# One graph and mixture-of-experts kernel: sorted groups of 13 and 4 blocks in place of 12 and 5, with earlier fills, later first tiles, and sums issued between the last sends

## The reference

```python
x = x + relu(adj @ (item_feat @ W_item.T + b_item) + layernorm(x) @ W_user.T + b_user)   # adj is 10000 x 10000
z = layernorm(x)
probs = softmax(z @ gate_w + gate_b)             # 8 experts
cw = the two largest of probs, zero elsewhere
x = x + sum over e of cw[:, e] * (gelu(z @ W1[e] + b1[e]) @ W2[e] + b2[e])
```

## Time and profile before

| what | value |
|---|---|
| median of three runs | 1503.61 us |
| profiled execution, its own time | 1498.51 us |
| its span in the profile | 1496.7 us |
| PE busy | 1451.1 us (97%) |
| DVE busy | 1262.9 us (84%) |
| ACT busy | 1093.5 us (73%) |
| POOL busy | 712.5 us (48%) |
| moved by DMA | 489.21 MB, 327 GB/s on average |
| TensorE clock granted, mean | 0.998 |

### The profile page before, as it was taken

One profiled execution on the slowest core, in us unless ns is written; L12 is line 12 of the kernel. 1 busy time (PEld: TensorE's weight loads), 2 busy tenths in 40 slices (PEclk: granted clock), 3 DMA queues, 4 the chain that ended last, 5 costly groups with the idle time before them and its releaser, 6 DMA issues.

```text
span 1496.7 us, 20455 instructions
## 1 busy us (share of the span) xinstructions
PE 1451.1 (97%) x6682; PEld 1165.6 (78%) x6682; DVE 1262.9 (84%) x1775; ACT 1093.5 (73%) x1162; POOL 712.5 (48%) x397
## 2 busy tenths in 40 slices
PE   8999999999999999999998999999999999999999
PEld 6778887887878887878876788888887777777676
DVE  5779889889889889898897789898888987788786
ACT  4667767767767777677674878787877777777675
POOL 0004434433442452453442276777576785676531
PEclk9999999999999999999999999999999999999999
DMA  9889999999999999999999999999898999877257
GB/s 337 315 309 361 375 390 363 377 382 354 378 381 355 375 382 362 379 370 371 374 342 326 343 340 314 350 321 350 314 338 300 319 326 330 295 251 264 92 117 151
DMA packets 126855, 489.21 MB, mean 327 GB/s; under 512 B 26320, under 2 KB 31736, under 8 KB 125662
## 3 DMA queue, kind: packets, MB, share of 16 engines
q1 hardware_dynamic: 114942, 457.21, 83.6%
q0 software_dynamic: 11808, 30.71, 6.8%
HBM read 455.77 MB, written 40.99 MB: 332 GB/s over the span
## 4 chain that ended last, share of the span: by engine, by line
PE 69%; DVE 12%; ACT 9%; issue 7%; DMA 2%; POOL 1%; SPq 1%; ACTq 0%; DVEq 0%; POOLq 0%
PE p_agg L476 17%; PE p_agg L471 16%; PE p_agg L472 15%; DVE s_a_lo L927 8%; ACT s_a_hi L717 4%; PE p_hid L564 2%; PE p_hid L566 2%; PE p_hid L565 2%; PE p_hid L453 2%; ACT s_xtok L733 2%; ACT s_rows L762 1%; PE p_y L580 1%; PE p_agg L487 1%; PE p_y L581 1%; PE p_y L582 1%
## 5 line engine op out<-in xcount | busy, mean ns | idle before, releaser
L927 DVE TENSOR_TENSOR s_a_lo<-s_raw,s_a_hi 128x1500 fp32r<-128x1500 f32 x520 | 884.4, 1718 | 113.2 <-PE p_agg L476 77.0
L717 ACT ACTIVATE s_a_hi<-s_raw 128x1500 fp32r<-128x1500 f32 x520 | 749.6, 1454 | 202.5 <-PE p_agg L476 188.3
L471 PE MATMUL p_agg<-s_a_hi,s_h_hi 128*128 128x500 f32 x1560 | 626.3, 401 | 4.7 <-ACT s_a_hi L717 4.7
L472 PE MATMUL p_agg<-s_a_hi,s_h_lo 128*128 128x500 f32 x1560 | 607.4, 389 | 0.0
L476 PE MATMUL p_agg<-s_a_lo,s_h_hi 128*128 128x500 f32 x1560 | 445.9, 394 | 13.0 <-DVE s_a_lo L927 9.6
L476 PEld LDWEIGHTS p_agg<-s_a_lo,s_h_hi 128*128 128x128 f32 x1560 | 287.1, 188 | 96.6 <-DVE s_a_lo L927 40.1
L1351 POOL DMA_INDIRECT rr<-s_ysb,s_dests x192 | 278.8, 1452 | 169.1 <-DVE s_ysb L1166 119.6
L471 PEld LDWEIGHTS p_agg<-s_a_hi,s_h_hi 128*128 128x128 f32 x1560 | 294.7, 189 | 64.0 <-ACT s_a_hi L717 6.4
L472 PEld LDWEIGHTS p_agg<-s_a_hi,s_h_lo 128*128 128x128 f32 x1560 | 294.9, 189 | 57.3 <-issue 3.2
L1342 POOL DMA_INDIRECT zs<-s_rows,s_idx x136 | 234.1, 1722 | 205.8 <-DVE s_idx L1085 157.2
L1318 POOL TENSOR_TENSOR s_gt<-s_ebase,s_gt 125x32 f32<-125x32 f32 x20 | 127.7, 6387 | 90.5 <-DVE s_gt L1011 87.0
(11 more groups left out here) (212 smaller groups left out, 1314.1 us busy)
## 6 DMA issues: line engine op xcount, KB each, us to landing
s_raw<-adj SPq DMA_DIRECT2D x520, 750.0 KB
s_wraw<-w SPq DMA_DIRECT2D x56, 256.0 KB
s_zt<-zs SPq DMA_DIRECT2D x48, 264.0 KB
out_s<-rr POOLq DMA_DIRECT2D x12, 512.0 KB, 10.9
s_xtok<-x_tok SPq DMA_DIRECT2D x20, 256.0 KB
s_xt<-x_t SPq DMA_DIRECT2D x20, 250.0 KB, 6.3
zs<-s_early SPq DMA_DIRECT2D x18, 264.0 KB, 7.0
out_s<-s_x1s SPq DMA_DIRECT2D x17, 256.0 KB, 7.0
```

What stands on the lines that cost most here:

```text
L471: mm(o, h_hi[:, k * D:(k + 1) * D], hi, start=(k == 0), stop=False)
L472: mm(o, h_lo[:, k * D:(k + 1) * D], hi, start=False, stop=False)
L717: fn(a_hi[:, n % HIS, :], raw[:, n % RAW, :], ACT.Copy).then_inc(hi_made, 1)
L927: tt(a_lo[:, n % LOS, :], raw[:, n % RAW, :], a_hi[:, n % HIS, :].bitcast(F32), ALU.subtract)\
```

## The change

Group 0 takes 13 blocks and group 1 takes 4. By the same formula group 0 has 33 tiles and group 1 has 15, still 48. Group 0's table comes a block later. Its W1 steps start at chunk 373 with a step of 104/33 = 3.15 chunks; group 1's start at 477 with a step of 41/15 = 2.73.

The fills start six chunks earlier against the table (at 362 and 466, that is (hi + 1) x 26 - 2) and wait for the first part of the table alone. The wait for the scatters, for the fills and for the whole table now stands at the first tile load of each group, at chunk 372 or 476 (FIRST_ZT). The weight loads of the first two dense experts move from the turns of chunks 517 and 518 to behind the last `load_raw`. Twelve of the fourteen adding transfers are issued between the last six sends, two behind each: rank 0 behind the sends of tiles 42 to 44, rank 1 behind those of tiles 45 to 47. The two for the last five blocks stay at the end. The scratch tile `gt` grows from 8 to 9 planes, since the table of 33 tiles needs 264 numbers.

```diff
-GROUPS = [(0, 12), (12, S)]
+GROUPS = [(0, 13), (13, S)]
...
-FILL_AT = [(hi + 1) * CH + 4 for lo, hi in GROUPS]
-FIRST_W1 = [at + E // 2 + 1 for at in FILL_AT]
+FILL_AT = [(hi + 1) * CH - 2 for lo, hi in GROUPS]
+FIRST_ZT = [(hi + 1) * CH + 8 for lo, hi in GROUPS]
+FIRST_W1 = [at + 1 for at in FIRST_ZT]
...
-W_LOAD = [0, 0] + [w + 5 for w in W1_AT[:NT - 2]] + [NCH - 3, NCH - 2]
-ZT_LOAD = [0, 0] + [max(W1_AT[k - 2] + 5, FILL_AT[k >= NTG[0]] + E // 2) for k in range(2, NT)]
+W_LOAD = [0, 0] + [w + 5 for w in W1_AT[:NT - 2]] + [NCH, NCH]
+ZT_LOAD = [0, 0] + [max(W1_AT[k - 2] + 5, FIRST_ZT[k >= NTG[0]]) for k in range(2, NT)]
...
-        gt = sb("gt", [P, 8, SUBS * E])
+        gt = sb("gt", [P, 9, SUBS * E])
...
                     sp.wait_ge(h_prod, CH + 1)
+                    sp.wait_ge(tab_made, 2)
+                if o == NTG[0]:
+                    sp.wait_ge(tab_made, 4)
...
                 if k == 0:
-                    sp.wait_ge(filled, 16 * E)
                     sp.wait_ge(spare_filled, 16 * 2)
-                if k == NTG[0]:
-                    sp.wait_ge(filled, 2 * 16 * E)
+                if k in (0, NTG[0]):
+                    g_ = int(k > 0)
+                    sp.wait_ge(tab_made, 2 * (g_ + 1))
+                    sp.wait_ge(scattered, 2 * 16 * SUBS * GROUPS[g_][1])
+                    sp.wait_ge(filled, 16 * E * (g_ + 1))
...
                 if e == 0:
-                    sp.wait_ge(scattered, 2 * 16 * SUBS * GROUPS[g][1])
-                    sp.wait_ge(tab_made, 2 * (g + 1))
+                    sp.wait_ge(tab_made, 2 * g + 1)
...
-                if n == FILL_AT[0] + E // 2:
+                if n == FIRST_ZT[0]:
...
-            load_w(NT + 2)
-            load_w(NT + 3)
+            for o in range(4):
+                load_w(NT + o)
...
-                first, last = (i * blocks, (i + 1) * blocks) if i < PAIRS else GROUPS[1]
+                first, last = (i * blocks, (i + 1) * blocks) if i < PAIRS else (PAIRS * blocks, S)
...
-                    pool.wait_ge(rank0_added, 16 * (PAIRS + 1))
+                    pool.wait_ge(rank0_added, 16 * (PAIRS + (i == PAIRS)))
...
                         send(k)
+                        i = k - (NT - PAIRS)
+                        if 0 <= i < PAIRS // 2:
+                            add_rank(2 * i, 0)
+                            add_rank(2 * i + 1, 0)
+                        elif i >= PAIRS // 2:
+                            add_rank(2 * i - PAIRS, 1)
+                            add_rank(2 * i - PAIRS + 1, 1)
...
-            for k in range(2):
-                for i in range(PAIRS + 1):
-                    add_rank(i, k)
+            add_rank(PAIRS, 0)
+            add_rank(PAIRS, 1)
```

More of the change, by code:

```diff
@@ L418, in _ @@
                         load_zt(k)
-                for o in range(2, NT + 2):
+                for o in range(2, NT):
                     if n == W_LOAD[o]:
```

## The result

| kernel | median of its runs | ratio to the kernel before | 95% interval |
|---|---|---|---|
| before | 1503.3 us (9 runs) | 1 | |
| changed | 1497.69 us (9 runs) | 0.9968 | 0.9957 to 0.9978 |
| changed, beside experiments 5 to 7 | 1497.37 us (6 runs) | 0.9958 | 0.9943 to 0.9973 |

The change makes the kernel about 5 us faster. The forecast was 9.5 us faster, 1494.1 us, with a range of 1483 to 1507. Sign and range hold, and the size is a little over half. The two profiled executions differ by only 1.5 us, 1498.51 and 1497.02 us. That of the kernel before had a granted clock of 0.998; its 44 timed runs beside the experiments have 0.992 to 0.997, most of them 0.994 or 0.995, and its profiled time is some 5 us under their median. So a profile is compared here by PE's idle time and by the clock column apart, and kernels by their timed runs.

What follows compares the result with a forecast made beforehand. PE, busy 97% of the span, was taken as the bound, so only its idle or half-clock time could be gained. Terms - 9 - 2.5 - 5 + 6 + 1 = - 9.5 us took 1503.6 to 1494.1 us, range 1483 to 1507.

Steps and rivals of the forecast that it cites:

- Item 1: First fills and tiles of group 0: earlier fills and the moved scatter wait gain 9 us, ends 0 and 12.1.
- My terms for tile 0: Group 0's first tile load: debt, weight loads, transfer, issues and landing put it 10 to 12 us after SP's turn.
- Item 2: Second gate, group 1's scatter wait at turn 472 moved to 476: 2.5 us gained, ends 0 and 5.
- Item 3: Blocks 18 and 19: thinner group 1 has fewer two-chunk W1 steps, 5 us gained, ends 0 and 8.
- Item 4: Denser group 0, 8.25 tiles a block: 1.5 us a block, 6 us lost; ends 0 and 24 lost.
- My line between two densities: PE idle in group 0: straight line from 6.2 to 10.8 tiles gives 2.85 us a block, 11 over four blocks.
- the remark that no step here is a two-chunk step: Group 0's W1 spacing: none of its steps is two chunks, which argues for less loss than the 11 us.
- Rival A: POOL decides: sends pushed behind scatters, low parts late in blocks 14 to 17, 24 us lost, time 1512; chance 0.16.
- Item 5: Adding transfers between the last sends: nothing gained at the end, 1 us lost, ends 0 and 6.
- item 6: The rest: later dense weight loads, table waits at `load_w`, larger table and dense steps, each priced at nothing.
- the signs that I gave for the after profile: Included: first-tile wait under 3 us, clock above 0.9 there, late PE idle halved, dense steps about 90 us.

Runs made afterwards that it cites:

- experiment 5: Kernel before with only the earlier fills and moved scatter wait, groups 12 and 5, sums at the end: ratio 0.9914, 13.0 us faster.
- experiment 6: Changed kernel (13 and 4) with sums at the end and one tiny early Gelu in block 1 to load ScalarE's table: ratio 0.9936 to the kernel before.
- experiment 7: Kernel before with earlier fills, moved wait and a tiny early Gelu, groups 12 and 5, sums at the end: ratio 0.9913, median 1490.41 us.
- experiment 4: Kernel before with groups of 13 and 4 alone; fills, waits, first tile and sums as before: ratio 0.9968, 5 us faster.
- experiment 1: Changed kernel with all fourteen adding transfers back behind the last send and the power: ratio 0.9938 to the kernel before, mean 1495.6 us.
- experiment 3: Changed kernel with groups of 12 and 5 instead of 13 and 4, moved wait and early sums kept: ratio 0.9946 to the kernel before.
- experiment 9: Changed kernel (13 and 4) with sums at the end and group 0's first tile three chunks later: ratio 0.9928 to the kernel before.
- experiment 2: Changed kernel with fills six chunks later and again behind the wait for scatters and whole table: ratio 0.9987 to the kernel before.
- experiment 10: Changed kernel with only the six rank 0 sums between the sends, rank 1 again at the end: ratio 0.9943 to the kernel before.

## Why the prediction was right in sign and half in size

**Item 1, the first fills (forecast: 9 gained).** The mechanism was right: the wait on SP went, ScalarE stood up to 2.7 us for a raw chunk but PE at most 1.0 behind it, the tile wait fell to 0.6 us. (My terms for tile 0 add up to 9 us, not to the 10 to 12 that I wrote, and 9 is nearer to what happened.) The size was off in this kernel. Idle and clock in blocks 12 to 14 went from 10.8 + 3.4 to 8.4 + 1.7 us, 4.1 gained; in timed runs the moved wait is worth 3.6 us at 13 and 4 (experiments 4 and 1) and 13.0 at 12 and 5 (experiment 5), both fills together. What I left out is the second gap, ScalarE's run of layer norm, table load and Gelu. It was in the earlier trace rows, among the 4.1 us that I put down to late raw loads, and neither the fills nor the wait touch it. At 3.15 chunks a tile it is longer (3.0 to 3.5 us with the moved wait, against 2.7 and 2.1 in experiments 3 and 5), because the next tile's rounding and weight split (lines 798 and 790 above) stand ahead of the next high part, where they come behind it at 12 and 5; and the clock fell behind it in every profile of 13 and 4 but that of experiment 9.

**Item 2, the second gate (2.5).** The tile waits of 3.8 us are gone and block 17 idles 1.6 us for 2.7, but not for the reason that I gave: both are so in experiment 4 too, where the gate was not moved. At 13 and 4 the grouping alone does it, and the moved gate takes no further idle time out of these blocks. At 12 and 5 the gate is worth the 2.0 us of block 18 (experiment 5), which is near my 2.5.

**Item 3, thinner group 1 (5).** Blocks 17 to 19 idle 12.1 us for 16.7, and the grouping alone brings 4.5 of these 4.6 us (experiment 4). For items 2 and 3 together I had 7.5. But it isn't my mechanism: apart from tile waits, blocks 18 and 19 idle 10.6 us for 10.3. Fewer two-chunk steps took the 5.1 us of `tile_turn` waits away, and PE's waits for high parts grew from 0.5 to 6.2 us in their place. With the wait moved first, thinning is worth 2.5 us (12.2 in experiment 1 for 14.8 in experiment 5). Why the late tiles went with the grouping was not tested.

**Item 4, denser group 0 (- 6).** The other way off: blocks 15 and 16 idle 1.6 us together. My line between two densities was wrong, and the remark that no step here is a two-chunk step was the better guide. Rival A, the sends, shows one step on: not at 13 and 4, but at 14 and 3. Items 3 and 4 together are + 1 in the forecast; measured alone, the grouping gives - 5.0 us (experiment 4).

**Item 5, early sums (- 1).** Mis-sized: 3 us at 13 and 4 and 4.8 at 12 and 5. What I priced, the raw loads and POOL's wait, is not where the profiles show it, but at two dense weights, for which ScalarE stands 4.2 and 2.3 us in the changed kernel. At 12 and 5 the dense steps grow by 5.5 us, which is all of it; at 13 and 4 by 1.1. I wrote "nothing" for such loads in item 6, since I looked only at their distance in chunks and not at what shares the queue: DMA stays 95% busy and more from 1400 to 1420 us.

**The sum** of measured parts, grouping - 5.0, moved wait - 3.6, sums + 3.1, is - 5.5 us, which is the changed kernel's mean against the mean of 1504.2 us beside experiments 1 to 4. It comes out by construction, since the three are steps of one path (experiments 4, 1, changed); by experiments 5 and 3 they are moved wait - 13.0, sums + 4.8, grouping + 2.7. My forecast for the three was + 1, - 11.5 and + 1: it missed them by 6.0, 7.9 and 2.1 us, and the first error hid most of the second. That the time lies in the range is in part luck. Of the signs that I gave for the after profile, all hold but three: PE's idle time in the last blocks did not halve, the dense steps are not about 90 us, and the clock at the first tiles is above 0.9 only as the block's mean (0.98), with 0.71 in one stretch of 5 us. I had not forecast that the clock takes part in nearly all of this. At full clock, 13 and 4 with the moved wait is the faster grouping (1488.1 against 1489.9 us, experiments 1 and 5); it loses 7.5 us of clock where 12 and 5 loses 1.2. So with the moved wait the regrouping still gains 1.9 us at full clock, and it is the clock that turns it into a loss. Which gaps make the clock fall isn't settled: in block 19 the same 5.1 us of idle had a clock of 0.98 in experiment 1 and 1.00 in experiment 4.

## What to carry to other kernels

When a wait is moved out of a queue, read the next gap behind it before pricing the gain: here an engine's burst, which I had put down to the same stall, kept 3.5 us of PE's 6.4 idle. A transfer moved "into idle DMA time" must be checked against every small load that shares the queue, also after the stage it was put in. And time the parts in both settings: regrouping gained 5 us alone and cost 4 once the wait was moved.

## What was not expected of the hardware

The length of a gap of PE alone does not tell whether the granted clock falls to half for some microseconds. It was low behind each gap of 3.0 to 5.0 us in blocks 13 and 14 (0.71 to 0.72 over the 5 us behind that of the changed kernel and the first of the earlier trace rows). But it also fell behind 2.0 us in the kernel before (0.66 in the earlier trace rows), 2.28 in experiment 6 (0.83) and 2.2 in experiment 3's dense steps (0.50), and in experiment 4 it was at 0.78 from 870 to 875 us, behind 1.95 us and ahead of the gap of 4.82, while it stayed at 1.00 behind 2.69, 2.10 and 1.54 us in block 13 of experiments 3, 5 and 7. Nor do all kernels keep one level from run to run: the two that lost least do (0.998 to 1.000, with a spread of 1.3 and 2.6 us between runs, experiments 5 and 7), but experiment 10's six runs go from a clock of 0.999 and 1491.65 us to 0.993 and 1499.3 us.

The Trainium skill (DMA: Bandwidth & Descriptors, section Queues, rings and completion order) says a DMA engine alternates packet by packet between queues with work. The late weights beside the adds agree with that (4.90 us of waiting for a 256 KB load in experiment 3, at most 0.4 in experiment 5), though no run measured the share itself.
